# Attention, experts, latent attention, experts on one core: VectorE adds one output tile between two rope operations

## The reference

```python
q = (q_latent @ Wqb)                      # 16 heads of 64 nope + 64 rope
r_even = x_even * cos - x_odd * sin       # rope of the 64 rope columns
r_odd = x_odd * cos + x_even * sin
kv = (c_kv @ Wkvb)                        # 64 nope keys + 128 values a head
scores = jnp.einsum('bhqd,bhkd->bhqk', q_full, k_full) * scale
probs = jax.nn.softmax(jnp.where(causal, scores, finfo.min))
attn = jnp.einsum('bhqk,bhkd->bhqd', probs, v)
x = x + out @ Wo
```

## Time and profile before

| | |
|---|---|
| median of 3 runs | 2430.17 us (2428.07 to 2433.02) |
| profiled execution | 2430.33 us |
| its span, first to last instruction | 2428.1 us |
| TensorE busy over the span | 2273.5 us, 94% |
| VectorE busy | 1825.1 us, 75% |
| ScalarE busy | 1206.4 us, 50% |
| GpSimd busy | 938.3 us, 39% |
| mean granted TensorE clock | 0.978 |

### The profile page before, as it was taken

How to read it: one execution, slowest core, us unless ns; L and a number is a source line. 1 busy time by engine, 2 the same in 40 slices (tenths; PEclk the granted TensorE clock), 3 DMA queues, 4 the chain that set the end, 5 groups by cost and what they waited for, 6 DMA issues and landing times. The chain is left out here.

```text
span 2428.1 us, 41872 instructions
## 1 busy us (share of the span) xinstructions
PE 2273.5 (94%) x12798; PEld 1949.8 (80%) x12798; DVE 1825.1 (75%) x4044; ACT 1206.4 (50%) x2803; POOL 938.3 (39%) x757
## 2 busy tenths in 40 slices
PE   6899999998999999889999789999999999889997
PEld 5788888887888888767887568888888888767786
DVE  6877777767777777766666748998999999975666
ACT  4555555554555555442333445666566566642334
POOL 5544444364344444345221332333343243234223
PEclk9999999999999999999999889999999999999998
DMA  5555555533333333215884100000000000017866
GB/s 177 194 194 193 193 193 193 191 128 109 114 109 112 114 114 114 98 65 211 307 280 180 58 19 1 19 19 0 18 19 18 0 18 18 18 60 272 281 232 232
DMA packets 106767, 296.61 MB, mean 122 GB/s; under 512 B 9480, under 2 KB 11912, under 8 KB 101024
## 3 DMA queue, kind: packets, MB, share of 16 engines
q1 hardware_dynamic: 85792, 239.59, 28.6%
q0 software_dynamic: 11360, 37.76, 4.1%
q10 hardware_dynamic: 9504, 17.85, 2.2%
HBM read 150.18 MB, written 144.98 MB: 122 GB/s over the span
## 5 line engine op out<-in xcount | busy, mean ns | idle before, releaser
L74 PE MATMUL bank<-xT_hi,w_hi 128*128 128x512 f32 x584 | 238.8, 409 | 38.2 <-issue 17.5
L74 PE MATMUL bank<-wo_hi,hq_hi 128*128 128x512 f32 x576 | 235.0, 408 | 15.4 <-DVE x L1419 13.7
L76 PE MATMUL bank<-xT_hi,w_lo 128*128 128x512 f32 x584 | 235.1, 403 | 0.0
L75 PE MATMUL bank<-xT_lo,w_hi 128*128 128x512 f32 x584 | 235.0, 402 | 0.0
L76 PE MATMUL bank<-wo_hi,hq_lo 128*128 128x512 f32 x576 | 226.4, 393 | 0.0
L75 PE MATMUL bank<-wo_lo,hq_hi 128*128 128x512 f32 x576 | 226.1, 392 | 0.0
L1489 POOL TENSOR_TENSOR qf<-ra,rb 64x512 f32<-64x512 f32 x64 | 82.5, 1289 | 337.4 <-DVE rb L1593 334.4
L823 DVE SCALAR_TENSOR_TENSOR x<-bank,inv,x 128x512 f32<-128x512 f32 x256 | 179.7, 742 | 21.9 <-PE bank L76 21.9
L1337 ACT ACTIVATE s<-s,top 128x128 f32<-128x128 f32 (+3 forms) x256 | 140.9, 552 | 95.0 <-DVE top L1411 94.8
L834 DVE TENSOR_TENSOR hq_lo<-bank,hq_hi 128x512 fp32r<-128x512 f32 (+1 forms) x144 | 80.3, 566 | 138.9 <-ACT arena L702 67.3
L1419 DVE SCALAR_TENSOR_TENSOR x<-bank,inv,x 128x512 f32<-128x512 f32 x256 | 179.8, 743 | 3.4 <-PE bank L76 0.4
(11 more groups left out here) (338 smaller groups left out, 7289.1 us busy)
## 6 DMA issues: line engine op xcount, KB each, us to landing
sorted_x<-blank SPq DMA_DIRECT2D x48, 1584.0 KB, 11.4
arena<-split_w SPq DMA_DIRECT2D x32, 1024.0 KB, 6.1
split_w<-arena SPq DMA_DIRECT2D x48, 512.0 KB, 3.1
w_raw<-dram_wa SPq DMA_DIRECT2D x32, 512.0 KB, 4.9
raw<-dram_wr SPq DMA_DIRECT2D x24, 512.0 KB, 6.1
wo_raw<-dram_woa SPq DMA_DIRECT2D x32, 256.0 KB, 4.0
ctok<-dram_wva SPq DMA_DIRECT2D x16, 512.0 KB, 5.1
arrived<-routed_y SPq DMA_DIRECT2D x8, 1024.0 KB, 8.0
```

Source lines behind the costliest of these rows:

```text
L74: nc.tensor.matmul(out, hi, mov_hi, start=first, stop=False)
L75: nc.tensor.matmul(out, hi, mov_lo, start=False, stop=False)
L76: return nc.tensor.matmul(out, lo, mov_hi, start=False, stop=last)
```

## The change

VectorE adds output tile 0 between the second and the third rope operation; tile 1 is added behind the third. `rope_out` is still raised by the third. `rotate` is now made of `rotate_parts`; its other use, in the latent stage, is as before.

```diff
         if new:
             dve.wait_ge(a.proj_done, s + 1)
             ge(dve, a.rope_added, s)
-            rotate(nc, m, m.bank[3]).then_inc(a.rope_out, 1)
+            rotate_parts(nc, m, m.bank[3], (0, 1))
         if n2:
             dve.wait_ge(a.inverted, v + 1)
-            add_output(v, bv, odd, (0, 1))
+            add_output(v, bv, odd, (0,))
+        if new:
+            rotate_parts(nc, m, m.bank[3], (2,)).then_inc(a.rope_out, 1)
+        if n2:
+            add_output(v, bv, odd, (1,))
         if n1:
             probs_lo(u)
...
+def rotate_parts(nc, m, bank, parts):
+
+    e, o = HALF, HALF + QUARTER
+    for part in parts:
+        if part == 0:
+            last = nc.vector.tensor_tensor(m.ra[e:P, :], bank[e:P, :], m.rope[e:P, 0, :], ALU.mult)
+        if part == 1:
+            last = nc.vector.tensor_tensor(m.rb[e:o, :], bank[o:P, :], m.rope[o:P, 1, :], ALU.mult)
+        if part == 2:
+            last = nc.vector.tensor_tensor(m.rb[o:P, :], bank[e:o, :], m.rope[e:o, 1, :], ALU.mult)
+    return last
```

More of the change, by code:

```diff
@@ L1585, in ge @@
         eng.wait_ge(sem, value)
+def rotate_parts(nc, m, bank, parts):
[8 more added lines that the diff above has]
+    return last
 def rotate(nc, m, bank):
[L1590 to L1593, removed]
+    return rotate_parts(nc, m, bank, (0, 1, 2))
 LATENT_BANK = [0, 1, 2, 5, 6]
```

## The result

The changed kernel takes 2445.55 us (median, 2442.67 to 2447.50) against 2430.17: a ratio of 1.0064, 95% interval 1.0053 to 1.0075. The change makes the kernel 15.4 us slower; 2446.3 was forecast. One of the five executions of the kernel before took 3209.84 us, where the other four lie between 2428.07 and 2433.02, and the ratio leaves it out. The profiled execution has a span of 2444.3 us, 16.2 over the one before. In the changed kernel the rope operations are lines 1597, 1599 and 1601, GpSimd's sum is 1493 and its remainder of the query 1503; the additions keep line 1419.

The account below looks back on a forecast made before the run. TensorE was taken to set the pace of the second attention, with VectorE having spare time. Terms of 5.2, 5.4, 1.1 and 4.4 us made 16.1 us slower, so 2446.3 us, range 2438 to 2451.

Parts of the forecast that it names:

- The bound and the place of the wait: Second attention: TensorE sets the pace; its wait before output tile 2 is not removed but moves to tile 3.
- The order's own cost: VectorE: third rope operation waits for the addition ahead to end, so it and rope_out come 0.77 us later.
- The overlap rival: VectorE: the addition overlaps with the third rope operation after all (0.66 us start to start); 2439.5 us, chance 0.15.
- Odd, b = 0: 7 steps: the combined product already waits for the third rope operation; 0.74 us net each, 5.2 us.
- Odd, b = 3: 7 steps, pairs 0 to 6: the query's remainder on GpSimd has no slack before the scores; 0.77 each, 5.4 us.
- Even, b = 0: 7 steps: the combined product's load comes 0.27 us later, its matmul 0.15; 1.1 us in all.
- Plain steps: 16 odd and 23 even steps: later query's remainder on GpSimd delays the scores; 0.09 and 0.13 us each, 4.4 us.
- The faster rival: TensorE's wait before tile 2 is truly gained: 12 us faster, 2418 us; chance 0.04.
- Nothing to measure: The addition overlaps and GpSimd's remainder is ready some 0.7 us before its span ends: 2432.7 us; chance 0.08.
- VectorE as a second bound: VectorE's cover before the reciprocal is gone: 0.10 us more in some 46 steps, 2451 us; chance 0.11.
- the chosen delivery times: Plain steps: remainder to scores' load taken as 0.08 us; with 0.05, both step losses are 0.03 less.
- the two steps of the last pair at b = 3: Last pair's b = 3 steps, where normalisation delays VectorE: counted at nothing.

Follow-up runs that it names:

- the second experiment: Against the kernel before: both tiles added between the second and third rope operation, so no output tile waits; 2485.56 us, ratio 1.0225.

## Why the prediction was right

*The bound and the place of the wait.* Right: the idle time sits between turning and the output tiles, and the second addition was as late as the first. The wait moved to tile 3 and was not removed. At the loads it is 0.98 us in odd steps, where some 0.7 were forecast as a sign; at the matmuls, 0.54, it is as long as before.

*The order's own cost.* Right: the third rope operation does not overlap with the addition. It comes 0.78 us later (0.77 forecast), tile 1's addition ends 0.12 later (0.10), since an addition alone takes 0.75 and the gaps are 0.03. The overlap rival, 2439.5, needed a start before 1737.32 and is refuted by the timeline. The Trainium skill (VectorE: DVE Perf Modes, section on two Vector instructions with no wait between them) says that an instruction whose input starts in another group of 32 partitions than the last read of that memory starts only when all earlier ones have finished. The trace agrees: the third rope operation starts 0.03 us after the end of the addition ahead of it, and the additions, which overlap when they stand together, no longer do. The prediction set the page's section on the DRAIN against this one. That section itself lets an instruction that is not held start earlier, so the two do not contradict each other.

*Odd, b = 0.* Right: 0.73 for 0.74. That it is rope_out ahead of the combined product is shown by moving the product: 0.61 of the 0.73 came back.

*Odd, b = 3.* Right in its cause, shown by the order on GpSimd; a little smaller, 0.72 for 0.77. The term had counted no slack, though rope_out came 0.78 us later and 0.72 arrived, so some 0.06 was there; the run of the kernel before with the other order fits, since the remainder held up 0.02 us at most.

*Even, b = 0.* 0.16 for 0.15; moving the combined product gave 0.10 of it back. The prediction and the description of the kernel leave out that GpSimd has a weight remainder ahead of the query's in these steps too (line 1327, 128x384, 1.02 us), in all pairs but the first. There was room for it: the query's remainder ended at 1786.47 with the scores' load at 1787.21 in the kernel before, and at 1796.17 with the load at 1796.30 in the changed one.

*Plain steps.* 0.15 and 0.10 for 0.13 and 0.09. In the odd step above, the second matmul of tile 3 comes 0.07 us later against the first rope operation, and the second of the scores 0.12. GpSimd's remainder in that step:

```profile
1740.20 1.29 POOL L1503 TENSOR_TENSOR hq_lo<-qf,hq_hi 128x512 fp32r<-128x512 f32 x1 [0.80 <-ACT hq_hi L1371]
```

It ends at 1741.49 and the scores' load follows at 1741.54. So about half seems to be tile 3 (0.05 forecast) and the rest GpSimd's remainder. This is read from the timeline; no run takes the two apart. The two odd plain steps of the first pair lost 0.29 us. There the scores' load comes 0.22 behind the end of the remainder and not 0.05, and why is open.

*The faster rival* fell with the result, and more clearly with the second experiment: with neither tile waiting, the kernel is 55.7 us slower. *Nothing to measure*, 2432.7, needed the overlap, which is not there, and a remainder that is ready sooner than its span ends; the scores waited 0.60 us for it at odd b = 3. *VectorE as a second bound* did not appear: its idle time before the reciprocal even grew, from 33.8 to 44.4 us.

The agreement within 1 us is partly luck: the chosen delivery times could have moved the plain steps by 0.03 each, over a microsecond in all, and the two steps of the last pair at b = 3, counted at nothing, vary by 3 us among the profiled executions.

## What to carry to other kernels

When a wait names one of two things produced back to back, look when the consumer gets the second: an earlier first one only moves the wait. Before putting an operation ahead of one that posts a semaphore, list everybody behind that semaphore and the slack of each; here the chain through three engines could take up some 0.65 of the 0.78 us in plain steps, under 0.1 where its queue had a second operation in front at odd b = 3, and the combined product at odd b = 0 could take up nothing. A wait that can't be shortened can be filled with work of the next step, up to the slack of the other engines.

## What the runs showed of the hardware

In these traces a VectorE operation whose partitions start elsewhere than those of the one ahead costs about 0.11 us more than its neighbours on the same partitions: 0.78 from start to start behind a 0.75 us addition, against 0.66 or 0.67 between operations on all partitions. It costs this on both its sides: the addition behind the third rope operation starts 0.03 us after its end. One and the same instruction shows both cases: the remainder of the keys starts 0.03 us after the end of the work ahead when it reads from partition 64, and 0.09 before that end when it reads from partition 0. Moving one such operation into a run of others therefore lengthens the run, though no instruction is added.
